# Four graph layers on one NeuronCore: the dense edge matrix holds (weight, gate) pairs and serves a fourth pass

## What is computed

```python
# third layer (L2): weighted sum over edges
h = x @ weight + bias
out = segment_sum(edge_weight[:, None] * h[src], dst, N)
# fourth layer (L3): three GCN layers with one gate per edge
ew = sigmoid(relu(edge_attr @ mw1 + mb1) @ mw2 + mb2)[:, 0]
deg = segment_sum(ew, dst, N) + 1.0
norm = rsqrt(deg)[src] * ew * rsqrt(deg)[dst]
h = x @ W + b
x = segment_sum(h[src] * norm[:, None], dst, N) + h / deg[:, None]
```

## Time and profile before

| what | us |
|---|---|
| runs: median (lowest to highest) | 7495.76 (7494.9 to 7497.09) |
| profiled execution: span of its trace | 7496.3 |
| POOL / PE / DVE / ACT busy over the span | 5305.8 / 5794.1 / 3503.5 / 1542.9 |
| scatter stage / weighted pass / three dense passes | 1600 / 1025 / 725, 710, 716 |

### The profile page before, as it was taken

How to read it: one execution, slowest core, us unless ns; L and a number is a source line. 1 busy time by engine, 2 the same in 40 slices (tenths; PEclk the granted TensorE clock), 3 DMA queues, 4 the chain that set the end, 5 groups by cost and what they waited for, 6 DMA issues and landing times. The chain is left out here.

```text
span 7496.3 us, 123067 instructions
## 1 busy us (share of the span) xinstructions
PE 5794.1 (77%) x30182; PEld 4263.8 (57%) x30182; DVE 3503.5 (47%) x13968; ACT 1542.9 (21%) x5084; POOL 5305.8 (71%) x5079
## 2 busy tenths in 40 slices
PE   3777777776628888867777766666699979998998
PEld 2444444445516555556666655555566656675665
DVE  4555555554446666645555533333222222232444
ACT  2333333331202222212222222222100000110001
POOL 3777777777657777657777567777577767776776
PEclk9888888887869999955555578999899999999998
DMA  8888888883224444423333234434477767766775
GB/s 262 185 153 160 156 157 152 153 151 118 89 74 117 116 116 117 108 69 84 83 77 83 72 110 117 118 118 117 154 245 235 238 191 241 241 214 216 242 243 178
DMA packets 693853, 1137.56 MB, mean 152 GB/s; under 512 B 139288, under 2 KB 441804, under 8 KB 691060
## 3 DMA queue, kind: packets, MB, share of 16 engines
q0 software_dynamic: 301456, 555.10, 33.1%
q1 hardware_dynamic: 389860, 552.91, 22.6%
q10 hardware_dynamic: 2304, 26.74, 0.8%
HBM read 889.84 MB, written 244.48 MB: 151 GB/s over the span
## 5 line engine op out<-in xcount | busy, mean ns | idle before, releaser
L900 POOL DMA_INDIRECT rows<-gcn_rows,index x1632 | 1547.9, 948 | 611.0 <-issue 466.2
L1434 POOL DMA_INDIRECT rows<-gat_rows,index x1568 | 1501.6, 958 | 642.8 <-issue 461.6
L1764 POOL DMA_INDIRECT support<-rows,index x784 | 1215.1, 1550 | 383.0 <-DMA support<-rows,index 219.7
L1565 PE MATMUL bank<-onehots,rows 128*128 128x128 f32 (+1 forms) x4704 | 945.8, 338 | 326.8 <-DVE rows L1641 326.6
L986 PEld LDWEIGHTS bank<-onehots,rows 128*128 128x128 f32 x6528 | 853.6, 193 | 421.3 <-issue 359.2
L1565 PEld LDWEIGHTS bank<-onehots,rows 128*128 128x128 f32 (+1 forms) x4704 | 721.2, 202 | 527.0 <-issue 327.3
L986 PE MATMUL bank<-onehots,rows 128*128 128x128 f32 x6528 | 882.1, 278 | 117.0 <-DVE onehots L1038 77.1
L676 POOL DMA_INDIRECT rows<-norm,index x784 | 742.6, 947 | 286.1 <-issue 225.1
L999 PE MATMUL dense_bank<-matrix,edge_space 128*128 128x512 f32 x1536 | 722.7, 593 | 0.0
L1881 PE MATMUL rows_bank<-x_window,cross 128*128 128x256 f32 x1568 | 615.1, 478 | 87.1 <-ACT cross L1865 86.8
L732 PE MATMUL bank<-onehots,rows 128*128 128x128 f32 x3136 | 485.9, 313 | 228.7 <-DVE onehots L763 204.1
(11 more groups left out here) (323 smaller groups left out, 8427.2 us busy)
## 6 DMA issues: line engine op xcount, KB each, us to landing
matrix<-matrix SPq DMA_DIRECT2D x96, 1024.0 KB, 7.0
edge_space<-gcn_rows SPq DMA_DIRECT2D x138, 512.0 KB, 9.5
alpha<-matrix SPq DMA_DIRECT2D x51, 1024.0 KB
dst_row<-in_dst_flat SPq DMA_DIRECT2D x100, 512.0 KB
source_row<-in_src_flat SPq DMA_DIRECT2D x99, 512.0 KB, 6.4
matrix<-zeros SPq DMA_DIRECT2D x196, 256.0 KB
support<-zeros ACTq DMA_DIRECT2D x16, 1632.0 KB, 28.0
rows<-gcn_rows,index POOLq DMA_INDIRECT x1632, 5.7
```

Source lines behind the costliest of these rows:

```text
L900: nc.gpsimd.indirect_dma_start(rows[:, k, :], None, table, bass.IndirectOffsetOnAxis(ap=index[:, k:k + 1], axis=0),).then_inc(gathered[k], 16)
L1434: nc.gpsimd.indirect_dma_start(rows[:, k, :], None, table, bass.IndirectOffsetOnAxis(ap=index[:, k:k + 1], axis=0),).then_inc(gathered[k], 16)
L1565: done = nc.tensor.matmul(to, left, onehots[:, k, :], start=first and c == 0, stop=final and c == chunks - 1)
L1764: nc.gpsimd.indirect_dma_start(support[k % COPIES], bass.IndirectOffsetOnAxis(ap=index[:, k // HALF, k % HALF:k % HALF + 1], axis=0), rows ...
```

## The change

The matrix in DRAM gets two floats an entry, the edge weights' sum and the gates' sum. The third layer runs as a `dense_pass` too, with value 0 of each pair, the fourth with value 1; `edge_pass` is gone. Dense matmuls read their moving operand with a step of two floats. Four-step buffers become a ring of seven one-step buffers of 512 KB, loaded one step at a time as each is used; the block's own loads are issued first. In the scatter stage each turn's comparisons are seven plain compares on DVE (same_edge), and PE multiplies them with the (weight, gate) pairs of seven neighbouring tiles, 15 matmuls of two columns a turn, in one PSUM bank; ACT copies the sums out. All repeats write the same sum, so the index correction is gone. Zeroing writes 512 KB for 256. In the block classes, sums or own rows that PE added by an identity matmul are now added by DVE.

```diff
-STEPS = 4
+SLOTS = 7
+LOW_SLOTS = 3
-TAIL_STEPS = 2 * TAIL_BATCH + 1
+NEAR = TAIL_BATCH + 2
@@ ScaledBlock
-    def pe_first(self, pe, s, j, b, runs):
...
-        pe.wait_ge(s.added, runs)
...
         for c in range(2):
-            to = by_chunk(self.turned)[:, c, :]
-            matmul(to, self.own_rows[:, c * P:(c + 1) * P], identity, start=c == 0, stop=False)
-            done = matmul(to, identity, self.g.acc[:, c, nodes_of(b)], start=False, stop=c == 1)
+            done = self.nc.tensor.matmul(by_chunk(self.turned)[:, c, :], self.own_rows[:, c * P:(c + 1) * P],
+                                         self.g.identity[:], start=c == 0, stop=c == 1)
...
+    def dve_first(self, dve, s, j, b, runs):
+        dve.wait_ge(s.turned, j + 2)
+        dve.wait_ge(s.added, runs)
+        here = by_chunk(self.turned)
+        self.nc.vector.tensor_tensor(here, here, self.g.acc[:, :, nodes_of(b)], ALU.add).then_inc(s.own_added, 1)
@@ WeightedBlock
-            matmul(to, self.sums[:, c, :], self.factor[:, c, :], start=c == 0, stop=False)
-        matmul(to, self.g.identity[:], x_of(self.g, b), start=False, stop=True).then_inc(s.multiplied, 1)
+            done = self.nc.tensor.matmul(self.product[:, 0:self.g.features], self.sums[:, c, :], self.factor[:, c, :],
+                                         start=c == 0, stop=c == 1)
...
+        self.nc.vector.scalar_tensor_tensor(x, self.bias[:], self.g.weight_sum[:, block_of(b)], x,
+                                            ALU.mult, ALU.add).then_inc(s.shifted, 1)
...
+        self.nc.vector.tensor_tensor(x, x, self.product[:, 0:self.g.features], ALU.add).then_inc(s.used, 1)
@@ LastBlock
-        matmul(to, identity, self.own_rows[:], start=True, stop=False)
...
+        self.nc.vector.scalar_tensor_tensor(x, self.own_rows[:], self.g.root_degree[:, block_of(b)], x,
+                                            ALU.mult, ALU.add).then_inc(s.own_added, 1)
@@ dense_pass
+    def stages_of(blocks_in_turn):
+        if ends.stages == 3:
+            return ((3, 9, 13),) if blocks_in_turn == 1 else ((2, 7, 9), (10, 14, 15))
+        return ((3, 9),) if blocks_in_turn == 1 else ((2, 6), (8, 13))
...
-        matrix = [g.matrix_space.rearrange("p (q n) -> p q n", n=GROUP),
-                  sbuf("matrix1", [P, STEPS, GROUP]), sbuf("matrix2", [P, STEPS, GROUP])]
+        high = sbuf("matrix", [P, SLOTS - LOW_SLOTS, 2 * GROUP])
+        matrix = [g.matrix_space[:, 2 * n * GROUP:2 * (n + 1) * GROUP] for n in range(LOW_SLOTS)]
+        matrix += [high[:, n, :] for n in range(SLOTS - LOW_SLOTS)]
...
+                def load_step(q):
+                    n, row = q % SLOTS, q % steps_of_group
+                    before = q - SLOTS
...
+                        sync.wait_ge(s.steps_used, before + 1 - before // steps_of_group)
+                    sync.dma_start(matrix[n], by_step[:, q, :]).then_inc(step_loaded[n], 16)
+                    sync.dma_start(table_rows[:, n, :], table[nodes_of(row), :]).then_inc(step_loaded[n], 16)
...
+                ends.sync_start(sync, s)
                 sync.wait_ge(g.matrix_written, 16 * (g.real_tiles - g.turns * RING))
-                for n in range(3):
-                    load_steps(n)
-                ends.sync_start(sync, s)
+                for q in range(SLOTS):
+                    load_step(q)
...
+                        done = nc.tensor.matmul(dense_banks[c][:, 0:GROUP], table_rows[:, n, c * P:(c + 1) * P],
+                                                matrix[n].rearrange("p (n v) -> p n v", v=2)[:, :, value],
+                                                start=row == 0, stop=row == steps_of_group - 1)
@@ scatter_by_source
                         sync.dma_start(matrix_steps[:, bass.ds(i, 1), q, :].rearrange("p i n -> p (i n)"),
-                                       zeros[:, 0:GROUP]).then_inc(g.matrix_zeroed, 16)
+                                       zeros[:, 0:2 * GROUP]).then_inc(g.matrix_zeroed, 16)
...
-                    gate = tail_gates[:, n:n + 1].to_broadcast([P, P])
-                    done = nc.tensor.matmul(gate_rows[:, n * P:(n + 1) * P], gate, g.identity[:], start=True, stop=True)
...
+                    for w in range(low, high + 1):
+                        done = nc.tensor.matmul(totals[:, w - 1, :], same_edge[:, r % 2, (w - low) * P:(w - low + 1) * P],
+                                                near_values[:, r, :], start=r == 0, stop=r == NEAR - 1)
...
-                        done = nc.vector.scalar_tensor_tensor(
-                            tail_scrap[:, v % 2, :], tail_row[:, v * P:(v + 3) * P], key,
-                            gate_rows[:, v * P:(v + 3) * P], ALU.is_equal, ALU.mult, accum_out=totals[:, v:v + 1])
...
+                    nc.vector.tensor_scalar(same_edge[:, r % 2, 0:(high - low + 1) * P], tail_row[:, low * P:(high + 1) * P],
+                                            g.tail_key[:, bass.ds(i * TAIL_BATCH + r, 1)], None, ALU.is_equal
+                                            ).then_inc(s.same_ready, 1)
@@ build_program
-    g.matrix = dram("matrix", [GROUPS * g.rows * P * GROUP, 1])
+    g.matrix = dram("matrix", [GROUPS * g.rows * P * GROUP, 2])
...
-        edge_pass(nc, g, norm2, edge_weight, WeightedBlock, factor=t.L2_gnn_weight, bias=t.L2_gnn_bias,
+        dense_pass(nc, g, norm2, 0, WeightedBlock, factor=t.L2_gnn_weight, bias=t.L2_gnn_bias,
                   keep=norm3, next_factor=t.L3_gnn_W1, next_bias=t.L3_gnn_b1, store=gcn[0])
...
-            dense_pass(nc, g, gcn[n], gate, ScaledBlock, own=gcn[n], factor=w, bias=b, store=gcn[n + 1])
+            dense_pass(nc, g, gcn[n], 1, ScaledBlock, own=gcn[n], factor=w, bias=b, store=gcn[n + 1])
```

More of the change, by code:

```diff
@@ L828, in ends_by_turn, with dense_pass @@
     return turns, rest
-def dense_pass(nc, g, table, weights, kind, **fields):
+def dense_pass(nc, g, table, value, kind, **fields):
     loops, batches = g.turns, RING // BATCH
@@ L837, in dense_pass, with place @@
     total = GROUPS * steps_of_group
-    loads = math.ceil(total / STEPS)
-    slots = GROUPS * GROUP_TURNS * RING
-    def slot(q):
-        return (q + 1) * slots // total - 1
+    places = GROUPS * GROUP_TURNS * RING
+    def place(q):
+        return (q + 1) * places // total - 1
     steps_after = {}
     for q in range(total):
-        steps_after.setdefault(slot(q), []).append(q)
-    def last_step(n):
-        return min((n + 1) * STEPS, total) - 1
-    def pieces(n):
-        at, end, parts = n * STEPS, last_step(n) + 1, []
-        while at < end:
-            to = min(end, (at // steps_of_group + 1) * steps_of_group)
-            parts.append((at, to))
-            at = to
-        return parts
-    in_buffer = {n: 16 * sum(1 + len(pieces(m)) for m in range(n % 3, n + 1, 3)) for n in range(loads)}
+        steps_after.setdefault(place(q), []).append(q)
+    weights = g.edge_values[:, :, value:value + 1].rearrange("p i a -> p a i")
     by_turn, rest = ends_by_turn(g)
@@ L1026, in _ @@
                 for j, b in enumerate(rest, len(g.order) - len(rest)):
-                    first(j, b, 2 * loops + 2)
-                    ends.pe_second(pe, s, j, b)
+                    ends.pe_first(pe, s, j, b)
+                    if ends.stages > 1:
+                        ends.pe_second(pe, s, j, b)
+                    if ends.stages > 2:
+                        ends.pe_third(pe, s, j, b)
             @block.vector
@@ L2131, in set_up @@
         hid = t.L3_gnn_mw2.shape[0]
-        with phase(nc, "loaded", "iota", "own", "relu", "added", "gated", "kept",
+        with phase(nc, "loaded", "iota", "own", "relu", "added", "gated", "weighted", "kept",
                    "turned", "wide", "zeros_ready", "keyed", "keys_kept") as (block, s):
@@ L2188, in _ @@
                 act.wait_ge(s.gated, 1)
-                nc.scalar.copy(g.tail_gate[:, 0:g.tiles - g.tail + 1], g.edge_values[:, g.tail - 1:, 1])
+                act.wait_ge(s.weighted, 1)
+                nc.scalar.copy(g.tail_pair[:, 0:g.tiles - g.tail + 1, :], g.edge_values[:, g.tail - 1:, 0:2])
             @block.tensor
@@ L3436, in build_program @@
         shares.append(dense_tiles - sum(shares))
+        writes, part = scoped()
+        g.matrix_index = part("matrix_index", [P, tiles - g.tail], INT32)
+        g.matrix_value = part("matrix_value", [P, tiles - g.tail, 2])
         inner, part = scoped()
@@ L3441, in build_program @@
             with ExitStack() as first:
+                g.tail_key = tiles_of(first, nc)[0]("tail_key", [P, tiles - g.tail + NEAR])
+                g.tail_pair = tiles_of(first, nc)[0]("tail_pair", [P, tiles - g.tail + NEAR, 2])
                 zeros = tiles_of(first, nc)[0]("zeros", [P, (blocks + 1) * features * COPIES // (2 * HALF)])
```

460 lines of the change are left out of this document (146 added, 314 removed).

## The result

The changed kernel takes 7629.49 us (median of 4 runs, 7624.4 to 7647.04) against 7496.43 us in the same comparison: ratio 1.018, 95% interval 1.0166 to 1.0195. It is 1.8% slower, clear of the spread of the runs; the forecast was 7296, range 7200 to 7430. The profiled execution has a span of 7622.7 us, 126.4 more than before.

What follows compares the result with a forecast made beforehand. POOL was taken to bound the scatter stage and the weighted pass, POOL and PE nearly level in dense passes. Terms -234 - 26 + 10 + 50 = -200 took 7496.3 to 7296 us, range 7200 to 7430.

Steps and rivals of the forecast that it cites:

- POOL covers it: Scatter stage: POOL's period hides 86 us of added PE work from narrow matmuls, so that work costs nothing.
- Rival 3: Scatter stage becomes DMA-bound through the doubled zeros: +156 us instead of +50, total 7400; chance 0.11.
- Weighted pass: Third layer run as a dense pass, gathers falling from 784 to 544: 783 us against 1017, -234; bounds -280 to -192.
- Middle passes: Two middle dense passes: sums moved off PE and block loads first bring POOL's pace, -13 us each, -26; bounds 0 and -30.
- Last pass: Last dense pass: PE's saving lies beside POOL and the own-row add costs nothing while POOL leads: 0 us.
- the matrix traffic: Dense passes: steps of 512 KB for 256 fit the DMA at 319 GB/s; +10 us over all passes, bounds 0 and +60.
- rival 2: Dense stages become DMA-bound at 300 GB/s: +150 us less 43 of hidden PE excess, total 7400; chance 0.12.
- the price of the zeros: Scatter stage: doubled zeroing writes, 51.4 MB more, lengthen POOL's waits by +50 us; bounds 0 and +156.
- the stages between: Set-up, index copies and 238 wider matrix writes are priced by POOL's instruction, not bytes: 0, at most a few us.
- rival 1: Dense matmuls' strided read is slow: doubled price gives about 8600 us; 15% more eats the 200 us gain; chance 0.09.
- the page's rule: Dense matmuls: two reads share each 16-byte line at an 8-byte step, so four passes stay at 1.72 us.
- POOL's idle time in the scatter stage: Sign expected in the scatter stage: POOL idle 433 us instead of 383, the stage's end at 1750 instead of 1700.

Runs made afterwards that it cites:

- s3: Kernel before, each zeroing load followed by a second 256 KB one into a spare array: scatter stage ends at 1767.6 us, 60 to 78 later than before.
- s1: Changed kernel with the key row's load issued after the first half's source row: scatter stage ends at 1783.6 us, ratio to before 0.9756.
- s5: Changed kernel with 7 instead of 15 narrow matmuls a turn (sums over neighbouring tiles left out): scatter stage ends at 1828.9 us, 175 to 184 earlier.
- e2: Changed kernel with each half's zeros issued behind its source row, key row's load left ahead: scatter stage ends at 1931.0 us, 82 earlier than after.
- s6: Changed kernel with key row's load moved behind the first source row and 7 narrow matmuls a turn instead of 15: scatter stage ends at 1786.5 us.
- s7: Kernel before with SP allowed to reload the key row after tile 15 instead of 13: scatter stage ends at 1682.4 us, against 1695.8 on that chip.
- d3: Changed kernel with key row's load moved, early one-hots and dense matmuls reading contiguous floats (wrong entries): passes take 773.7, 712.3, 711.4 and 698.7 us.
- d2: Kernel before with the block's loads issued ahead of the matrix in dense passes: middle passes take 718.7 and 719.6 us, ratio 0.9984.
- e1: Changed kernel with key row's load moved, early one-hots, zeros behind source rows and an earlier last-pass store: 7352.49 us, ratio to before 0.9786.
- v1: Changed kernel with key row's load moved and four of the next turn's one-hots made before the last block's second part: ratio to before 0.9831.

## Why the prediction was wrong

**The scatter stage** is the step that failed: "POOL covers it: its period is 1.85 us a tile, PE's busy time 1191/784 = 1.52, then 1.63". Of the 326 us between forecast and result, 255 lie here. The step compares averages over the stage. A turn is a cycle through SP, a load, DVE and PE, and the change put PE's sums and a late compare into it. Then it takes 39 us in the mean (1905/49), 41 in the turn shown, where POOL's 16 scatters need 29.6. The forecast priced 15 narrow matmuls as PE time beside other work; they are followed by DVE's compare, and this by the head of SP's queue. The wait for source_row, 288 us before, was already in the trace, and I took no row of it, since no engine that bounds waited for it.

The loss of 305 us divides so: 60 to 78 for the bytes of the zeros (s3; 67 remain in the last version, 1774.2 - 1707.4, and 74 to 102 stay in the three with the key row moved and the zeros not), and the rest, some 235 by s3, for the cycle (s1: 220 to 229). Within the cycle each link is worth its time: the key row's wait 220 to 229 us (s1), half of the sums 175 to 184 (s5), 512 KB ahead of the source row 73 to 85 (e2). They do not add, since each of them alone shortens the same turn, and at some 1780 us the scatters and bytes bound the stage (s6). The late key row alone costs nothing in before (s7). Rival 3 named this stage at half the loss; its mechanism is wrong, since the DMA share fell. The rivals contained no cycle.

PE's clock belongs to it. It was granted at 0.84 of full in this stage before and 0.75 after. In the turn above PE begins after its wait at the lower of the two levels, 1.2 GHz (granted 0.50 from 924.5 to 933.5 us), and goes over to the higher later (1.00 from 935 to 939). In before it did the same after waits of 2.6 and 3.6 us: 0.56 from 928 to 934, 0.98 from 934 to 944. A tile takes 928.00 - 925.74 = 2.26 us in the first stretch and 936.26 - 935.02 = 1.24 in the second (timeline of PE):

```profile
925.74 0.80 PE L1751 MATMUL cross_bank<-same_source,onehots 128*128 128x128 f32 x2
...
928.00 0.63 PE L1751 MATMUL cross_bank<-same_source,onehots 128*128 128x128 f32 x2
...
935.02 0.47 PE L1751 MATMUL cross_bank<-same_source,onehots 128*128 128x128 f32 x2
...
936.26 0.38 PE L1751 MATMUL cross_bank<-same_source,onehots 128*128 128x128 f32 x2
```

But in s7, where PE waits longer than in before (428.0 us for DVE, 314.1 in before), the clock was 0.86, and in s1, where it waits less than in after, 0.79. So which part of the 235 us is the clock's was not shown.

**Weighted pass**: -204 for -234, inside the bounds (-280 to -192). The tail was right, 60.5 for 58. The miss is in the turns with two blocks: first to last gather 752.8 us for 725; they take 24.9 us or more, of which PE's work is 22.1 and 0.5 for the stride, and the waits for one-hots and for ACT's sums are 1.4 and 1.2 (18.8/13, 14.7/12). The waits are as large as forecast, 2.5; that half of them would be covered was wrong. Three of these turns take 28.0 to 29.6 us, and why is open. The stride is worth 12 us of the pass by d3.

**Middle passes**: -2 for -26, just inside. Both effects were found (first turn 20.0 us, adds off PE), and neither arrived: d2 shows the first given back in later turns where PE leads, and the stride put 16 us on PE where the adds took off 22. Taking the stride away gave 17.0 and 11.6 us in these two passes (d3 against e1), enough for the 24 us missed, though a pass moves by up to 11 us with its code unchanged. The term rested on turns with one block (19.0 us); those with two need 20.3 of PE by the same prices, and 20.8 with the stride, over POOL's 20.0.

**Last pass**: +29 for 0. The forecast said that its turns run at POOL's pace and priced the own-row add alone. It missed a queue: the store now waits on SP behind one-step loads, each of which waits for PE; DVE needs that store before the second block's first part and makes the one-hots behind it. By e1 the store's place is worth 14 us on one chip (684.6 against 698.7 in d3 and 698.0 in e2), 18 against v1; with it moved, 4 us of the loss are left.

**Right**: the matrix traffic fits (rival 2 is out), the price of the zeros (50 forecast, 60 to 78 in s3), nothing on the stages between. Of rival 1 the mechanism is real and its size 5%, a third of the 15% at which it decides; the page's rule (the Trainium skill, "SBUF — State Buffer", Specifications (TRN2), Cachelines: two reads a line keep full bandwidth) would have had 1.72 us, and the trace shows 1.80.

**Sums that do not come out**, without weight for the result: rival 2's 4 x 32 x 1.3 is 166, not 150; the weighted pass's upper bound of 765 is 680 + 27 + 65 = 772 if each turn with two blocks loses 5 us more; and the two middle passes come 14 and 11 us down to 683, 25 in sum. Of the signs, POOL's idle time in the scatter stage was to be 433 us and was 691.9.

## What to carry to other kernels

Where a loop's period is set by several engines, follow one turn around: which instruction frees a buffer, which queue waits for that at its head, what stands behind it, who needs that. Averages of busy time do not show such a cycle, and a wait that costs nothing today can be its first sign. When a change makes an early releaser depend on a later engine, move its reload behind the loads that others need; here that single line of order was worth 220 us, more than the 204 us that the change gained in the weighted pass. And when large loads become many small ones that each wait, look at what else shares their queue.

## What was not expected of the hardware

A moving operand read with a step of 8 bytes costs 5% in a 512-column float32 matmul (1.80 against 1.72 us for four passes), not nothing and not double; some 190 steps of a middle pass show the same two times. And on two of the chips used the same program needed 8913 to 8917 us for 7494 to 7509: the scatter stage alike (1689.3 and 1707.4), the weighted pass 1315 for 1017, the first dense pass 860 for 722. The change itself comes out 1.8% slower on one chip and equal (1.0015) on another, and a total read on one against a total from the other says nothing.
